# A graph network's expert layer: scatters and gathers of 25 blocks written out, a running sum by one scan, batch norm in five parts

## The chip, the cores and the metric

One Trainium2 chip, one of its cores. The metric is the device time of one execution of the whole kernel in microseconds (us). The engines are TensorE (PE; PEld is its weight load), VectorE (DVE), ScalarE (ACT), GpSimd (POOL) and SyncE (SP); each has its own instruction stream, and they meet through semaphores. DMAs are issued by SP and by POOL.

## The reference, cut to what matters

Four graph layers follow each other on 3125 nodes with 256 features, each added to its input: weighted means, a mixture of experts, four attention layers by angle, three graph attention layers. The change touches only the second. There `x` (3125 x 256) is what each node's feed-forward part starts from:

```python
logits = x @ Wg + bg                        # 64 experts
vals, idx = jax.lax.top_k(logits, TOP_K)    # 2 for each node
gates = jax.nn.softmax(vals, axis=-1)
order = jnp.argsort(e_flat)                 # nodes sorted by expert
rank = jnp.arange(N * TOP_K) - offs[e_s]    # place of a node within its expert
buf = zeros.at[slot].set(x[tok_s])          # rows to the experts
h1 = gelu(buf @ w1 + b1); h2 = h1 @ w2 + b2
core = zeros.at[tok_s].add(g_s[:, None] * y_s)   # rows back, weighted by the gate
y = x + core
mean = jnp.mean(y, axis=0)
var = jnp.mean((y - mean) ** 2, axis=0)
out = (y - mean) * jax.lax.rsqrt(var + BN_EPS) * gamma + beta
```

## The kernel before

The nodes lie in `NB = 25` blocks of 128 on the partitions; the last block has `LAST = 53` of them. `k.X` [128, 25, 256] is the sum that runs through the layers, `k.Y` of the same shape the `x` of this layer and later its `y`. A stage of the kernel is a block of code for all engines; between two blocks stands a barrier, so that a stage is as long as its slowest chain, and what one stage saves is not waited away in the next.

`route` (its first block) finds the two experts of each node on DVE, in tiles of 128 x 1600 (25 blocks x 64 experts). `cnt` holds a 1 where a node goes to an expert. TensorE multiplies it by `k.tri` (how many earlier nodes of the same block go there: `pre`) and by ones (how many of the block: `tot`). DVE copies both out of PSUM, and L1259 to L1262 is a loop in which each pass adds one block's totals to the sum of the blocks before, with a wait behind every addition. L1265 adds that sum to the rank. From the rank follow `slot_put` and `slot_get`, the row numbers in the experts' buffers in DRAM.

The second block of `route` scatters the rows of `Y` to the buffer `xbuf`. DVE copies a block's rows and its two columns of row numbers to a ring of `RING = 5` slots (L1332, L1333), because inside the loop the block number is a register; POOL issues two indirect DMAs for each block (L1342).

`experts` works on 112 tiles of 128 rows and writes `ybuf`. It is not changed.

`combine` is one block of code. DVE copies the row numbers of five blocks to `frm` (L1555), and the wait ahead of these copies is for all additions of the five blocks before. POOL gathers two rows for each node from `ybuf` to the ring `row` (L1544). DVE multiplies them by the gate and adds them to `Y` (L1561, two for each block). When all 50 additions are done, PE sums `Y` over the nodes by 25 products with ones (L1590, L1592); DVE takes the mean off `Y` (L1567), ACT squares `Y` to `acc` (L1581), PE sums the squares in the same way, DVE makes the factor `var` from it (L1569 to L1573), and three passes over 128 x 6400 elements end the layer: times `var` (L1574), plus beta (L1575, `aff[:, 1, :]`), and onto `X` (L1576). SP fetches gamma and beta at the start of the block (L1535). The next stage, a layer norm of `X` (L570), begins behind the barrier.

## Time and profile before

| | us |
|---|---|
| time, median of 2 runs | 8447.11 (8445.72 to 8448.5) |
| the profiled execution's own time | 8452.29 |
| span of the profiled execution | 8450.6 |
| busy: PE, DVE, POOL, ACT | 5775.2, 5350.2, 5261.2, 2998.2 |
| mean granted TensorE clock | 0.888 of full speed |

The span runs from the first to the last instruction. The busy times are sums over the whole span, and no engine is busy for more than 68% of it: the stages have different limits. The stages that the change touches lie between 2432 and 3198 us of the span, that is, 766 us with the experts (some 460 us) between them.

### The profile page before, as it was taken

To read this page: it belongs to the slowest core of one execution; us is meant where nothing else is said; L and a number is where in the kernel's file an instruction comes from. 1 tells how busy PE (TensorE), PEld (TensorE's weight loads), DVE (VectorE), ACT (ScalarE), POOL (GpSimd) and SP (SyncE) were. 2 spreads that over 40 slices of the span, in tenths; PEclk is the share of its full clock that TensorE was granted. 3 is DMA by queue.
4 is the path that set the end of the run, shared out by engine and by line. 5 is a ranking of instruction groups with operands and counts; after the bars stand their busy time and mean duration, and the time that the engine had idled before them with its cause. 6 is when DMAs were issued, how large, how long until landed. Compare 5 with 4: busy or idle time off the path is not lost. (4 is left out here: it accounts for less than half of the span.)

```text
span 8450.6 us, 153428 instructions
## 1 busy us (share of the span) xinstructions
PE 5775.2 (68%) x32873; PEld 4645.0 (55%) x33057; DVE 5350.2 (63%) x15356; ACT 2998.2 (35%) x7461; POOL 5261.2 (62%) x5324
## 2 busy tenths in 40 slices
PE   0005445546547945997997997898588878887886
PEld 0004435534336844776776776777366656655664
DVE  8003346664441227777776777777688868887888
ACT  0001100000012214444444444444466646655664
POOL 4777777757712125776776776776367646656764
PEclk9996677767778977999999999999799989999998
DMA  6001123323308942343443443443233323323332
GB/s 228 10 2 47 53 70 102 103 80 104 103 24 295 370 153 81 105 106 101 105 105 100 105 105 100 105 106 96 69 93 94 89 78 93 93 74 94 94 92 72
DMA packets 597889, 866.01 MB, mean 102 GB/s; under 512 B 273775, under 2 KB 412013, under 8 KB 596374
## 3 DMA queue, kind: packets, MB, share of 16 engines
q0 software_dynamic: 233280, 595.84, 25.6%
q1 hardware_dynamic: 364502, 269.16, 10.6%
q14 instruction: 90, 0.74, 0.0%
q8 instruction: 17, 0.28, 0.0%
HBM read 740.80 MB, written 125.75 MB: 103 GB/s over the span
## 5 line engine op out<-in xcount | busy, mean ns | idle before, releaser
L1766 POOL DMA_INDIRECT hs<-tab_agnn,rec x1952 | 1900.1, 973 | 653.6 <-issue 559.2
L2209 POOL DMA_INDIRECT hs<-tab_gat,rec x1464 | 1521.7, 1039 | 680.1 <-issue 417.2
L1832 DVE CUSTOM_DVE_ANT_0 prod<-psG,hs 128x256 f32<-128x256 f32 x1952 | 829.1, 481 | 404.9 <-DMA hs<-tab_agnn,rec 324.2
L1895 PE MATMUL psG<-HN,ohT 128*128 x3904 | 966.1, 391 | 12.8 <-DVE lg L1832 5.8
L2241 DVE TENSOR_REDUCE mt<-psL 128x2 f32<-128x1024 f32 x732 | 860.0, 1215 | 142.9 <-PE psL L2362 84.8
L1912 PE MATMUL psV<-hs,pr 128*128 128x258 f32 x3904 | 934.0, 383 | 0.0
L1895 PEld LDWEIGHTS psG<-HN,ohT 128*128 128x128 f32 x3904 | 710.6, 192 | 107.7 <-issue 20.3
L1849 ACT ACTIVATE prT<-cand,mn 128x512 f32<-128x512 f32 x488 | 352.4, 722 | 1170.2 <-DVE mn L1792 1157.9
L1912 PEld LDWEIGHTS psV<-hs,pr 128*128 128x128 f32 x3904 | 707.8, 191 | 80.9
L2378 PE MATMUL psV<-msg,oh 128*128 128x260 f32 x2928 | 730.4, 394 | 1.0 <-DVE msg L2286 0.6
L805 PE MATMUL psT<-ident,oh 128*128 128x128 f32 x416 | 101.6, 391 | 847.8 <-DVE oh L770 847.8
L2378 PEld LDWEIGHTS psV<-msg,oh 128*128 128x128 f32 x2928 | 580.0, 198 | 131.2 <-issue 9.1
L2362 PE MATMUL psL<-sT,sel 128*128 128x512 bf16 x1464 | 572.2, 391 | 15.8 <-DVE mt L2241 3.5
L805 PEld LDWEIGHTS psT<-ident,oh 128*128 128x128 f32 x416 | 65.2, 194 | 875.3 <-DVE oh L770 825.9
L2361 PE MATMUL psL<-neg,identb 128*128 128x512 bf16 x1281 | 500.7, 391 | 54.4 <-DVE mt L2241 54.4
L529 POOL DMA_INDIRECT rec_d<-R x392 | 397.8, 1015 | 215.1 <-issue 215.1
L657 POOL DMA_INDIRECT hs<-tab_gc,rec x416 | 406.9, 978 | 195.0 <-issue 122.9
L697 PE MATMUL ps<-hs,oh 128*128 128x256 f32 x832 | 316.8, 547 | 287.1 <-DMA hs<-tab_gc,rec 258.2
L875 POOL DMA_INDIRECT hs<-tab_bwd,rec x416 | 420.5, 1011 | 134.3 <-issue 125.4
L750 POOL DMA_INDIRECT fwd_d<-msg,rec x416 | 408.9, 983 | 141.9 <-issue 79.8
L2305 ACT ACTIVATE away<-iotas,rec 128x128 bf16 x1464 | 462.3, 386 | 92.3 <-DMA rec<-rec_d 57.5
L2286 DVE TENSOR_TENSOR msg<-hs,msg 128x1024 f32<-128x1024 f32 x366 | 451.4, 1233 | 5.4 <-ACT msg L2317 1.8
(346 smaller groups left out, 12120.4 us busy)
## 6 DMA issues: line engine op xcount, KB each, us to landing
w<-in_L_gnn_w SPq DMA_DIRECT2D x224, 512.0 KB, 6.0
hs<-tab_agnn,rec POOLq DMA_INDIRECT x1952
fwd_d<-acc SPq DMA_DIRECT2D x10, 2730.0 KB, 34.1
fw<-fwd_d SPq DMA_DIRECT2D x104, 260.0 KB, 2.8
hs<-tab_gat,rec POOLq DMA_INDIRECT x1464
rec<-rec_d SPq DMA_DIRECT2D x1166, 10.0 KB, 1.8
b<-in_L_gnn_b SPq DMA_DIRECT2D x113, 128.0 KB, 6.4
x<-xbuf SPq DMA_DIRECT2D x112, 128.0 KB, 6.0
```

The costliest lines, as they stand in the source:

```text
L875: nc.gpsimd.indirect_dma_start(out=hs[:, j, g, :], out_offset=None, in_=k.tab_bwd, in_offset=bass.IndirectOffsetOnAxis(ap=rec[:, j, g, 0:1 ...
L1766: nc.gpsimd.indirect_dma_start(out=hs[:, j, g, :], out_offset=None, in_=k.tab_agnn, in_offset=bass.IndirectOffsetOnAxis(ap=rec[:, j, g, 0: ...
L1832: ins = V.tensor_tensor_reduce(prod[:, h2, g, :], psG[:, bank(j2, half), m, :], hs[:, j2, g, 0:D], hs[:, j2, g, D:D + 1], 0.0, ALU.mult, A ...
L1895: mm = nc.tensor.matmul(psG[:, bank(j1, half), m, :], ohT[:, j1 % 2, 2 * half + m, :], pick(HN, b, slice(None)).rearrange("p a c -> p (a c ...
L1912: mm = nc.tensor.matmul(psV[:, j5 % 2, 0:cols], pr[:, j5 % 2, g, :], hs[:, j5, g, 0:cols], start=(g == 0), stop=(g == G - 1))
L2209: nc.gpsimd.indirect_dma_start(out=hs[:, j, g, :], out_offset=None, in_=k.tab_gat, in_offset=bass.IndirectOffsetOnAxis(ap=rec[:, j, g, 0:1 ...
L2241: V.tensor_reduce(mt[:, h2, m:m + 2], psL[:, m:m + 2, :], AX.X, ALU.max).then_inc(s_lt, 1)
L2286: V.tensor_tensor(hmsg[:, :, :, 0:C_HEAD], hrow[:, :, :, 0:C_HEAD], hmsg[:, :, :, C_HEAD].unsqueeze(3).to_broadcast([P, G, HEADS, C_HEAD]) ...
L2305: ins = nc.scalar.activation(away[:, j, g, :], nodes, ACT.Abs, bias=recf[:, j, g, 4:5], scale=-1.0)
L2361: nc.tensor.matmul(psL[:, m, :], k.identb[:, :], neg[:, h2, :], start=True, stop=False)
L2362: mm = nc.tensor.matmul(psL[:, m, :], sel[:, m, :], sT[:, h2, :], start=False, stop=True)
L2378: mm = nc.tensor.matmul(psV[:, h5, 0:W_GAT], oh[:, h5, g, :], msg[:, h5, g, :], start=(g == 0), stop=(g == G - 1))
```

## The change

In the first block of `route` the loop of additions goes. `tots` and `run` lie with the blocks innermost, DVE copies the totals there from PSUM in four pieces of 7, 7, 7 and 4 blocks, and one scan over 1600 elements multiplies the sum so far by `goes_on` (0 at an expert's first block, 1 elsewhere) and adds the next total. The scan's sum includes the block itself; `below = tri - 1` takes the place of `tri` and subtracts it again. `rank` is added up straight from PSUM, in four pieces. New at the start of the block are the instructions that write `below` and `goes_on`.

In the second block of `route` and in `combine` the loops over blocks are written out. The indirect DMAs take rows and row numbers from `Y`, `slot_put` and `slot_get` themselves; the copies of DVE are gone. In `combine` POOL waits, from the sixth block on, only for the two additions of the block five before.

Batch norm: beta is added to `X` at the start of `combine`. PE adds a block to the first sum as soon as the block's additions are done. Taking off the mean, squaring, the sum of squares, the product with `var` and the addition onto `X` go in five parts of five blocks.

```diff
-                c.mark(V.tensor_copy(sv(rank), pv(pre)))
-                c.mark(V.tensor_copy(sv(tots), pv(tot)))
-                with dve.Fori(0, NB) as b:
-                    V.tensor_tensor(pick(run, b + 1, slice(None)), pick(run, b, slice(None)), pick(tots, b, slice(None)),
-                                    ALU.add).then_inc(s_chain, 1)
-                    dve.wait_ge(s_chain, b + at + 1)
-                c.done(V.tensor_tensor(rank[:, :, :], rank[:, :, :], run[:, 0:NB, :], ALU.add))
+                c.mark(V.tensor_scalar(below[:, :], k.tri[:, :], 1.0, None, ALU.subtract))
+                c.done(V.memset(goes_on[:, :, :], 1.0))
+                c.mark(V.memset(goes_on[:, :, 0], 0.0))
...
+                for n in range(NC):
+                    c.mark(V.tensor_copy(tots[:, :, chunk(n)].rearrange("p e b -> p b e"), of(tot, n)))
+                dve.wait_ge(s_chain, c.n)
+                c.done(V.tensor_tensor_scan(flat(run), flat(goes_on), flat(tots), 0.0, ALU.mult, ALU.add))
+                for n in range(NC):
+                    c.mark(V.tensor_tensor(rank[:, chunk(n), :], of(pre, n), run[:, :, chunk(n)].rearrange("p e b -> p b e"), ALU.add))
...
+                for b in range(NB):
+                    if b >= RING:
+                        pool.wait_ge(s_put[b % RING], b // RING * 32)
+                    for m in range(TOP_K):
+                        nc.gpsimd.indirect_dma_start(
+                            out=k.xbuf, out_offset=bass.IndirectOffsetOnAxis(ap=k.slot_put[:, b, m:m + 1], axis=0),
+                            in_=k.Y[:, b, :], ...).then_inc(s_put[b % RING], 16)
...
+                for b in range(NB):
+                    if b >= RING:
+                        pool.wait_ge(s_add, TOP_K * (b - RING + 1))
+                    for m in range(TOP_K):
+                        nc.gpsimd.indirect_dma_start(
+                            out=row[:, b % RING, m, :], out_offset=None, in_=k.ybuf,
+                            in_offset=bass.IndirectOffsetOnAxis(ap=k.slot_get[:, b, m:m + 1], axis=0)).then_inc(s_get[b % RING], 16)
...
+                dve.wait_ge(s_gb, 32)
+                c.mark(V.tensor_tensor(k.X[:, :, :], k.X[:, :, :], mid(aff[:, 1, :], NB), ALU.add))
...
+                for n in range(RING):
+                    V.tensor_tensor(k.Y[:, parts[n], :], k.Y[:, parts[n], :], mid(mean[:, :], NB // RING), ALU.subtract).then_inc(s_part, 1)
...
-                c.done(V.tensor_tensor(Yf, Yf, mid(aff[:, 1, :], NB), ALU.add))
...
+                for n in range(RING):
+                    act.wait_ge(s_part, n + 1)
+                    nc.scalar.activation(k.acc[:, parts[n], 0:D], k.Y[:, parts[n], :], ACT.Square).then_inc(s_sq, 1)
...
+                for b in range(NB):
+                    pe.wait_ge(s_add, TOP_K * (b + 1))
+                    mm = total(0, b, k.Y)
```

On DVE in the first block of `route`, before:

```order
L1254 COPY rank<-pre 128x1600
L1255 COPY tots<-tot 128x1600
L1256 MEMSET run 128x64
L1259 UNCONDITIONAL_BRANCH
L1259 ISA
L1260 ISA
L1260 TENSOR_TENSOR run<-run,tots 128x64
L1262 REGISTER_ALU
L1259 REGISTER_ALU
L1259 COMPARE_AND_BRANCH
L1265 TENSOR_TENSOR rank<-rank,run 128x1600
```

and with the change:

```order
L1261 COPY tots<-tot 128x7x64 x3
L1261 COPY tots<-tot 128x4x64
L1263 SCALAR_TENSOR_TENSOR run<-goes_on,tots 128x1600
L1265 TENSOR_TENSOR rank<-pre,run 128x448 x3
L1265 TENSOR_TENSOR rank<-pre,run 128x256
```

The loop body, which ran 25 times, is gone, and the scan (it is listed under the name of its instruction family) stands between the four copies and the four additions; `rank` is written once instead of twice.

On POOL the scatter's stage, before (the ten DMAs are one pass of a loop of five):

```order
L1337 UNCONDITIONAL_BRANCH
L1337 ISA
L1342 DMA xbuf<-row,to 14336x256 x10
L1337 REGISTER_ALU
L1337 COMPARE_AND_BRANCH
```

and with the change:

```order
L1323 UNCONDITIONAL_BRANCH
L1329 DMA xbuf<-Y,slot_put 14336x256 x50
L1321 UNCONDITIONAL_BRANCH
```

The 50 scatters stand one behind the other, and read what DVE's copies used to stand between. The gathers of `combine` change in the same way (L1544 x10 in a loop to L1530 x50).

On DVE from the start of `combine` to its end, with the change:

```order
L1539 TENSOR_TENSOR X<-X,aff 128x6400
L1545 SCALAR_TENSOR_TENSOR Y<-row,gate,Y 128x256 x50
L1548 TENSOR_SCALAR mean<-ps 128x256
L1551 TENSOR_TENSOR Y<-Y,mean 128x1280 x5
L1553 TENSOR_SCALAR var<-ps 128x256
L1555 RECIPROCAL var<-std 128x256
L1556 TENSOR_TENSOR var<-var,aff 128x256
L1559 TENSOR_TENSOR Y<-Y,var 128x1280 x5
L1562 TENSOR_TENSOR X<-X,Y 128x1280 x5
```

where before, behind the additions, stood:

```order
L1566 TENSOR_SCALAR mean<-ps 128x256
L1567 TENSOR_TENSOR Y<-Y,mean 128x6400
L1569 TENSOR_SCALAR var<-ps 128x256
L1571 RECIPROCAL var<-std 128x256
L1573 TENSOR_TENSOR var<-var,aff 128x256
L1574 TENSOR_TENSOR Y<-Y,var 128x6400
L1575 TENSOR_TENSOR Y<-Y,aff 128x6400
L1576 TENSOR_TENSOR X<-X,Y 128x6400
```

The pass with beta moved from between the last two passes to ahead of all additions, and the other three are each five instructions.

## Rows read from the trace of the kernel before

**Rows 1.** Busy time by stretch: us, then each engine's busy us (instructions), clock, DMA

```profile
3045.50:3132.40 86.90, 0.00 (x0) 0.00 (x0) 28.17 (x75) 0.00 (x0) 49.41 (x50) 0.50 0.27 79
```

**Rows 2.** Timeline of DVE in the route: start, us, engine, line, operation, idle before

```profile
2466.56 1.82 DVE L1254 COPY rank<-pre 128x1600 f32<-128x1600 f32 x1 [6.32 <-PE tot L1304]
...
2471.44 0.22 DVE L1260 TENSOR_TENSOR run<-run,tots  x1 [0.56 <-DVE run L1260]
...
2491.26 0.20 DVE L1266 TENSOR_SCALAR ne<-run 128x64 f32<-128x64 f32 x1
```

**Rows 3.** Groups by line and shape: busy us, mean ns, idle before

```profile
L452 DVE TENSOR_TENSOR_SCAN scan<-onesj,carry,mask 128x296 f32<-128x296 f32 x50 | 39.0, 822 | 4.6 <-DVE prod L456 4.1 <-DVE R L472 0.5
L452 DVE TENSOR_TENSOR_SCAN scan<-onesj,offs,mask 128x96 f32<-128x96 f32 x50 | 18.2, 405 | 5.2 <-DVE carry L459 4.8 <-DVE prod L441 0.4
L664 DVE MEMSET acc<- 128x6500 f32 x1 | 5.5, 5475 | 12.6 <-issue 12.6
```

**Rows 4.** Timeline of DVE at the start of the experts

```profile
2587.68 0.61 DVE L1429 COPY b1T<-psx 128x256 f32<-128x256 f32 x1 [19.96 <-PE psx L1472]
...
2589.07 0.42 DVE L1443 COPY xT<-psx 128x256 f32<-128x256 f32 x1
```

**Rows 5.** Timeline at the start of the scatter's stage

```profile
2512.20 0.21 DVE L1290 TENSOR_TENSOR slot_put<-slotf,okf 128x50 int32<-128x50 f32 x1
...
2513.77 0.16 DVE L1333 COPY to<-slot_put 128x2 int32 x1
...
2514.87 1.02 POOL L1342 DMA_INDIRECT xbuf<-row,to  x1 [82.00 <-DVE to L1333]
```

**Rows 6.** Groups of the page's part 5: the scatters of the sorting stage

```profile
L529 POOL DMA_INDIRECT rec_d<-R x392 | 397.8, 1015 | 215.1 <-issue 215.1
```

**Rows 7.** Timeline of that stage

```profile
504.35 0.97 POOL L529 DMA_INDIRECT rec_d<-R  x1 [0.30 <-issue]
```

**Rows 8.** Groups by line between 3045 and 3133 us: the gathers

```profile
L1544 POOL DMA_INDIRECT row<-ybuf,frm x50 | 49.4, 988 | 45.1 <-DVE frm L1555 18.9 <-issue 13.7 <-SPq L1530 12.5
```

**Rows 9.** Timeline of combine: start, and the end of the first five blocks

```profile
3045.58 0.43 SPq L1535 DMA_DIRECT2D aff<-in_L_gnn_beta  x1
3046.58 1.01 POOL L1544 DMA_INDIRECT row<-ybuf,frm  x1 [12.55 <-SPq L1530]
...
3058.44 0.95 POOL L1544 DMA_INDIRECT row<-ybuf,frm  x1 [0.31 <-issue]
...
3061.98 0.49 DVE L1561 SCALAR_TENSOR_TENSOR Y<-row,gate,Y 128x256 f32 x1 [0.15 <-DVE Y L1561]
```

**Rows 10.** DMA issues: KB each, us from issue to landing

```profile
aff<-in_L_gnn_beta SPq DMA_DIRECT2D x1, 128.0 KB, 3.0
```

**Rows 11.** Timeline of graph attention: DVE and POOL at the same time

```profile
6498.79 1.22 DVE L2286 TENSOR_TENSOR msg<-hs,msg 128x1024 f32<-128x1024 f32 x1
6499.19 1.64 POOL L2209 DMA_INDIRECT hs<-tab_gat,rec  x1 [0.30 <-issue]
```

**Rows 12.** Timeline of the batch norm

```profile
3132.46 1.22 PE L1590 MATMUL ps<-Y,ones 53*128 53x256 f32 x2 [100.16 <-DVE Y L1561]
3146.55 0.42 DVE L1566 TENSOR_SCALAR mean<-ps 128x256 f32<-128x256 f32 x1 [14.14 <-PE ps L1592]
...
3159.46 1.22 PE L1590 MATMUL ps<-acc,ones 53*128 53x256 f32 x2 [12.94 <-ACT acc L1581]
...
3173.78 0.42 DVE L1569 TENSOR_SCALAR var<-ps 128x256 f32<-128x256 f32 x1 [19.94 <-PE ps L1592]
...
3183.86 6.83 DVE L1575 TENSOR_TENSOR Y<-Y,aff 128x6400 f32<-128x6400 f32 x1
```

**Rows 13.** Busy time by stretch, within the first sum on PE

```profile
3140.00:3147.00 7.00, 6.52 (x31) 5.40 (x29) 0.42 (x1) 0.00 (x0) 0.00 (x0) 1.00 0.00 0
```

**Rows 14.** Parts of five blocks in the attention by angle

```profile
3243.37 7.10 DVE L1698 TENSOR_TENSOR HN<-H,rnb 128x1280 f32<-128x1280 f32 x5
```

**Rows 15.** Groups of ACT between 3220 and 3245 us

```profile
L1706 ACT ACTIVATE HN<-H 128x1280 f32<-128x1280 f32 x5 | 6.4, 1270 | 3.7 <-DVE H L1683 3.5
```

More of the change, by code:

```diff
@@ L1190, in route @@
         rank = sb("rank", X3)
-        tots = sb("tots", X3)
-        run = sb("run", [P, NB + 1, EXPERTS])
+        tots = sb("tots", [P, EXPERTS, NB])
+        run = sb("run", [P, EXPERTS, NB])
+        goes_on = sb("goes_on", [P, EXPERTS, NB])
+        below = sb("below", [P, P])
         top = sb("top", [P, 2, NB])
@@ L1301, in _ @@
                 for n in range(NC):
-                    r = flat(cnt)[:, n * CH:(n + 1) * CH]
-                    nc.tensor.matmul(pre[:, n, 0:CH], k.tri[:, :], r, start=True, stop=True)
-                    mm = nc.tensor.matmul(tot[:, n, 0:CH], k.ones[:, 0:P], r, start=True, stop=True)
+                    r = cnt[:, chunk(n), :].rearrange("p b e -> p (b e)")
+                    nc.tensor.matmul(pre[:, n, 0:wide(n)], below[:, :], r, start=True, stop=True)
+                    mm = nc.tensor.matmul(tot[:, n, 0:wide(n)], k.ones[:, 0:P], r, start=True, stop=True)
                 mm.then_inc(s_pre, 1)
@@ L1512, in combine @@
         sem = lambda n: ctx.enter_context(nc.semaphore(tagged(nc, n)))
-        s_from = [sem(f"s_from{n}") for n in range(RING)]
         s_get = [sem(f"s_get{n}") for n in range(RING)]
@@ L1528, in combine @@
         ps = ctx.enter_context(nc.psum_tensor(tagged(nc, "ps"), [P, 2, 512], F32))
-        Yf = k.Y[:, :, :]
+        parts = [slice(n * (NB // RING), (n + 1) * (NB // RING)) for n in range(RING)]
         with nc.Block() as block:
@@ L1538, in _ @@
             def _(pool):
-                with pool.Fori(0, NB // RING) as i:
-                    for n in range(RING):
-                        pool.wait_ge(s_from[n], i + 1)
+                for b in range(NB):
+                    if b >= RING:
+                        pool.wait_ge(s_add, TOP_K * (b - RING + 1))
                         pool.sem_inc(s_gate, 1)
-                        for m in range(TOP_K):
-                            nc.gpsimd.indirect_dma_start(
-                                out=row[:, n, m, :], out_offset=None, in_=k.ybuf,
-                                in_offset=bass.IndirectOffsetOnAxis(ap=frm[:, n, m:m + 1], axis=0)).then_inc(s_get[n], 16)
+                    for m in range(TOP_K):
+                        nc.gpsimd.indirect_dma_start(
+                            out=row[:, b % RING, m, :], out_offset=None, in_=k.ybuf,
+                            in_offset=bass.IndirectOffsetOnAxis(ap=k.slot_get[:, b, m:m + 1], axis=0)).then_inc(s_get[b % RING], 16)
             @block.vector
@@ L1571, in _ @@
                 c.done(V.reciprocal(var[:, :], std[:, :]))
-                dve.wait_ge(s_gb, 32)
                 c.done(V.tensor_tensor(var[:, :], var[:, :], aff[:, 0, :], ALU.mult))
-                c.done(V.tensor_tensor(Yf, Yf, mid(var[:, :], NB), ALU.mult))
-                c.done(V.tensor_tensor(Yf, Yf, mid(aff[:, 1, :], NB), ALU.add))
-                c.done(V.tensor_tensor(k.X[:, :, :], k.X[:, :, :], Yf, ALU.add))
+                dve.wait_ge(s_part, RING)
+                for n in range(RING):
+                    V.tensor_tensor(k.Y[:, parts[n], :], k.Y[:, parts[n], :], mid(var[:, :], NB // RING), ALU.mult).then_inc(s_part, 1)
+                for n in range(RING):
+                    dve.wait_ge(s_part, RING + n + 1)
+                    c.mark(V.tensor_tensor(k.X[:, parts[n], :], k.X[:, parts[n], :], k.Y[:, parts[n], :], ALU.add))
             @block.scalar
             def _(act):
-                act.wait_ge(s_bn, 2)
-                nc.scalar.activation(k.acc[:, :, 0:D], Yf, ACT.Square).then_inc(s_sq, 1)
+                for n in range(RING):
+                    act.wait_ge(s_part, n + 1)
+                    nc.scalar.activation(k.acc[:, parts[n], 0:D], k.Y[:, parts[n], :], ACT.Square).then_inc(s_sq, 1)
                 act.wait_ge(s_bn, 3)
@@ L1586, in _, with total @@
             def _(pe):
[L1588 to L1593 removed]
+                def total(n, b, src):
+                    lo = LAST if b == NB - 1 else P
+                    return nc.tensor.matmul(ps[:, n, 0:D], k.ones[0:lo, 0:P], src[0:lo, b, 0:D], start=(b == 0), stop=(b == NB - 1))
+                for b in range(NB):
+                    pe.wait_ge(s_add, TOP_K * (b + 1))
+                    mm = total(0, b, k.Y)
+                mm.then_inc(s_sum, 1)
+                for b in range(NB):
+                    if b % (NB // RING) == 0:
+                        pe.wait_ge(s_sq, b // (NB // RING) + 1)
+                    mm = total(1, b, k.acc)
+                mm.then_inc(s_sum, 1)
 def attention_by_angle(nc, k, a):
```

65 lines of the change are left out of this document (16 added, 49 removed).

## The prediction

> **What bounds the kernel now.** The kernel is a row of stages with barriers between them, so I read the stages that the change touches one by one and ask in each for the chain that ends last. The view by stretches comes first [rows 1]: while rows come back from the experts (86.9 us), POOL is busy for 49.4 us, DVE for 28.2 us and PE not at all. Nobody is full; waits set the time. In the route the timeline shows a chain on DVE alone: from the copy of `pre` at 2466.56 to the first use of the finished sum at 2491.26, 24.7 us, most of it additions of 0.22 us with 0.5 to 0.6 us of waiting ahead of each [rows 2]. In the gathers the chain is POOL's: 50 DMAs of 0.988 us with 0.30 us of issue between them, and four waits of together 18.9 us for `frm` [rows 8]. Behind the last addition (3132.4) PE's sum, the mean, the squares, PE's second sum and three long passes of DVE stand one behind the other [rows 12].
>
> **The change part by part.**
>
> *Running sum.* 24.7 us go. New: four copies out of PSUM. A piece adds a fixed cost; 1600 elements took 1.82 us in one [rows 2], five pieces of 1280 took 7.10 us [rows 14] where 6400 in one took 6.83 [rows 12], so about 0.07 us for each cut: 2.0 us. Four additions from PSUM, the same 2.0. The scan: 296 elements took 822 ns and 96 took 405 [rows 3], so 2.09 ns an element, and 1600 make 3.5 us. With three waits 7.6 us. At the start of the block `below` and `goes_on` are new and nothing hides them, since the chain waits behind them: 6500 elements of memset took 5.48 us [rows 3], so 1600 take 1.4, and with two small instructions 1.8 us. Gain 24.7 - 7.6 - 1.8 = 15.3. The copies now write with a stride of 100 bytes, which no large instruction before does. The nearest row is a copy out of PSUM that writes with a stride of 16 bytes: 0.61 us for 256 elements against 0.42 with none [rows 4]; that may be the stride or not. Taken over to 1600 elements, for copies and additions, it costs at most 2.4 us; at least it costs nothing. I take nothing, and keep 2.4 for the range. PE's products have the same number of columns.
>
> *Scatter.* POOL sets the stage: one scatter follows the other, and DVE's copies run beside them. Scatters that are written out stand elsewhere in this kernel, 392 of them, and come 1.27 us apart, 0.97 busy and 0.30 issue [rows 6, 7]. So only the start counts. Before, the row numbers were copied at 2513.93 and POOL began 0.94 us later; the last instruction of the block before ended at 2512.41 [rows 5]. Without copies POOL starts from the barrier, which lies between, and still needs its 0.94 us: gain 1.0, bounds 0 and 1.5.
>
> *Gathers.* Waits of 18.9 us for `frm` go, and the ring does not take their place: a block is added 3.1 us after POOL has issued it (3059.39 to 3062.47, [rows 9]), and POOL comes back to the slot 10 us later. But DVE now begins with beta onto `X`, 6.83 us [rows 12], as soon as beta is there: 3045.58 + 3.0 = 3048.6 [rows 9, 10], until 3055.5. It has both inputs in SBUF. What such an instruction does to POOL stands in another stage: DVE's addition from 6498.79 to 6500.01, and a gather that was to start in the middle of it, at 6499.19, took 1.64 us instead of the 0.94 to 0.95 of its neighbours, so it was held until about 0.1 us before DVE's end [rows 11]. Here two or three gathers start before 3048.6; the next one is held until 3055.4, ends at 3056.35, and its successor starts at 3056.65. If three have started before, 46 remain: 46 x (0.988 + 0.304) = 59.4 [rows 8], the last ends at 3115.8. The additions end 3.1 us later in the shown five [rows 9], but in the last of the five fives 3.9 (the last gather there was issued from 3127.61 on), so I take 3.3: 3119.1, against 3132.4. With one gather more to go it is 3120.4. Middle of both: gain 12.6.
>
> The Trainium skill, "SBUF — State Buffer", section "Who interferes with whom", says that a DVE instruction with two SBUF inputs contends with a GpSimd instruction that reads SBUF, and that whichever comes first holds the port for its whole length. This case's trace agrees (1.64 us, rows 11). The same section reports that `tensor_tensor` did not stall DMA in an earlier probe; by that the hold would be nothing and the sum 5.8 us larger, which is the first rival below.
>
> *First sum.* PE added 25 blocks behind the last addition: 3132.46 to 3146.55, 14.1 us [rows 12]. Now 24 of them lie under the gathers (a block each 2.6 us, even at the low clock 0.9 us of PE) and the last costs the 1.22 us of its first pair [rows 12]: gain 12.8.
>
> *Squares.* Before, mean to `var` took 27.2 us [rows 12]. Now the first part is 0.42 + 1.5 us on DVE, 1.27 on ACT [rows 15], then PE's 25 blocks, which took 14.3 us [rows 12] and need about 2.1 (high clock) to 4.3 us (low) for a part, while the next part arrives after 1.4: PE never waits long, and its sum sets the end: 0.5 + 1.5 + 1.3 + 14.3 = 17.6. Gain 9.6. This keeps the clock's course: PE began at a low clock, and within the sum it was raised; in the first sum the mean of 3140 to 3147 was 1.00, that is 2.4 GHz, and 31 products took 6.52 us, 0.21 each [rows 13].
>
> *End.* The pass with beta, 6.83 us, is gone from here; two passes in five parts cost 0.27 us more each [rows 12, 14]: gain 6.3.
>
> Sum: 15.3 + 1.0 + 12.6 + 12.8 + 9.6 + 6.3 = 57.6 us. The profiled execution took 8452.3 us as a whole (span 8450.6): it would take 8394.7. The median of the two runs is 5.2 lower, so 8389.5 there.
>
> **The rivals.**
>
> - The hold does not happen, so that beta's pass is free. The gather that starts at about 3049.6 ends at 3050.6 and not at 3056.35: 5.8 us more gain, 8384. Against it: the gather that was held in the other stage [rows 11]. Chance 0.12.
> - PE stays at the low clock for the sum of squares, since its work before is now in small pieces, and five-block parts may leave gaps. Each product would take 0.43 instead of 0.21, 50 of them 21.3 instead of 14.3: 7 us less gain, 8396. Against it: from the first square on PE has a queue. Chance 0.12.
> - The strided copies or the scan cost more, or part of a saved wait comes back in a barrier or in the next layer's start: 5 to 15 us less, 8395 to 8405. Chance 0.12.
> - Slower than before: instructions that are written out are fetched from DRAM once each, while a loop's are at hand. If POOL stalls at this, 100 indirect DMAs pay. It decides from 0.58 us for each DMA (57.6 / 100); at 1 us each the time is 8389 + 100 = 8489. For it speaks only that the issue in rows 6 has a mean of 0.55 us, with the waits for the sorting in it. Against it: 392 written-out scatters at 1.27 us [rows 7]. Chance 0.02, also for ending above 8447.
> - The change does not do what it says (the wait for the ring bites as `frm` did): POOL would wait again for 18.9 us, 8408. Against it: the 10 us of slack. Chance 0.02.
>
> **How the numbers follow.** The forecast has chance 0.6, with 8380 to 8399 as its own range (stride 2.4, start 1.5, one gather 1.3, the clock's rise a few us earlier or later, 3 us between runs). The range that holds 8 in 10 takes in the first two rivals and most of the third: 8376 to 8404. A measurement of this kernel can tell about 2% from no change, which is 169 us. All of what these stages could give is less: the touched stretches sum to about 25 + 73 + 87 + 65 us, and POOL's 100 DMAs alone keep 127 of them. Faster by over 2%: 0.01. Slower by over 2%: 0.01. Within: 0.98.
>
> **What would show it.** In the profile of the changed kernel: a scan of 3.5 us between four copies and four additions, each group 2.0 us; scatters at 1.27 us with DVE idle; beta onto `X` at about 3032 (3048.6 less the 16.3 us saved before), and one gather beside it of 5 to 7 us instead of 1; no wait of POOL for DVE's additions; the mean 1.3 us behind the last addition; `var` 17.6 us behind the mean; 14.2 us for the last ten passes. A mean gather duration of 1 us with none above 2 would prove the hold wrong; a gap above 0.5 us between written-out DMAs would prove the price of written-out code wrong; and if the stages save 57 us but the time does not, what lies behind them has changed, which no row here foretells.

## The result, and the profile after

The changed kernel takes 8361.55 us (median of 2 runs, 8360.1 to 8363.0) against 8447.11 before: 0.9898 of it, 95% interval 0.988 to 0.9915. That is 85.6 us less, where 57.6 were forecast; the forecast of 8389.5 (8376 to 8404) lay 28 us above the measured time. The profiled executions, which the sum was made against, differ by 92.2 us in their spans.

The page of after, its first lines (span; busy time of each engine, share, instructions):

```profile
span 8358.4 us, 152930 instructions
## 1 busy us (share of the span) xinstructions
PE 5760.2 (69%) x32873; PEld 4634.0 (55%) x33057; DVE 5311.7 (64%) x15276; ACT 3000.4 (36%) x7465; POOL 5337.3 (64%) x5324
```

The route, as in [rows 2]: a timeline of DVE with start, us, engine, line, operation, names and the idle time ahead.

```profile
2465.49 2.98 DVE L1261 COPY tots<-tot 128x448 f32<-128x448 f32 x4 [7.56 <-PE tot L1305]
2468.50 3.49 DVE L1263 TENSOR_TENSOR_SCAN run<-goes_on,tots 128x1600 f32<-128x1600 f32 x1
2472.03 3.15 DVE L1265 TENSOR_TENSOR rank<-pre,run 128x448 f32<-128x448 f32 x4
2475.22 0.22 DVE L1267 TENSOR_SCALAR ne<-run 128x64 f32<-128x64 f32 x1
```

From the first copy to the first use of the sum 9.73 us pass, before 24.7. The scan takes the 3.5 us forecast; the copies and additions take 2.98 and 3.15, not 2.0 each.

The start of the scatters, as in [rows 5]:

```profile
2496.16 0.21 DVE L1291 TENSOR_TENSOR slot_put<-slotf,okf 128x50 int32<-128x50 f32 x1
2497.96 1.01 POOL L1329 DMA_INDIRECT xbuf<-Y,slot_put  x1 [69.39 <-PEq L1321]
2499.28 1.00 POOL L1329 DMA_INDIRECT xbuf<-Y,slot_put  x1 [0.31 <-issue]
```

The start of the gathers, as in [rows 9]:

```profile
3029.38 0.43 SPq L1521 DMA_DIRECT2D aff<-in_L_gnn_beta  x1
3029.72 1.01 POOL L1530 DMA_INDIRECT row<-ybuf,slot_get  x1 [11.89 <-POOLq L1376]
3031.04 0.99 POOL L1530 DMA_INDIRECT row<-ybuf,slot_get  x1 [0.30 <-issue]
3032.34 0.95 POOL L1530 DMA_INDIRECT row<-ybuf,slot_get  x1 [0.30 <-issue]
3032.64 6.82 DVE L1539 TENSOR_TENSOR X<-X,aff 128x6400 f32<-128x6400 f32 x1 [16.07 <-DMA aff<-in_L_gnn_beta]
3033.59 6.70 POOL L1530 DMA_INDIRECT row<-ybuf,slot_get  x1 [0.30 <-issue]
3039.39 1.00 DVE L1545 SCALAR_TENSOR_TENSOR Y<-row,gate,Y 128x256 f32<-128x256 f32 x2
...
3040.59 0.94 POOL L1530 DMA_INDIRECT row<-ybuf,slot_get  x1 [0.30 <-DVE Y L1545]
```

The hold of the forecast is there in full: the fourth gather starts while DVE adds beta and takes 6.70 us. And the batch norm, as in [rows 12] and [rows 14]:

```profile
3100.50 1.00 DVE L1545 SCALAR_TENSOR_TENSOR Y<-row,gate,Y 128x256 f32<-128x256 f32 x2 [2.30 <-DMA row<-ybuf,slot_get]
...
3102.81 0.42 DVE L1548 TENSOR_SCALAR mean<-ps 128x256 f32<-128x256 f32 x1 [1.31 <-PE ps L1577]
3103.27 7.10 DVE L1551 TENSOR_TENSOR Y<-Y,mean 128x1280 f32<-128x1280 f32 x5
...
3119.88 0.42 DVE L1553 TENSOR_SCALAR var<-ps 128x256 f32<-128x256 f32 x1 [9.51 <-PE ps L1577]
...
3123.10 7.10 DVE L1559 TENSOR_TENSOR Y<-Y,var 128x1280 f32<-128x1280 f32 x5
3130.12 7.09 DVE L1562 TENSOR_TENSOR X<-X,Y 128x1280 f32<-128x1280 f32 x5
```

The mean starts 1.31 us behind the last addition, `var` 17.07 us behind the mean.

To place the 92.2 us I cut every trace at the starts of certain instructions of POOL: its first iota of the route, the first scatter, the first gather of `combine`, the iota behind it, the first gather of the attention by angle, the iota behind its last gather, and the first and last gathers of the graph attention. The short stretches ahead of "by angle" and on both sides of "graph att." are in no column, and so the delay of p2_before_delay, which lies in the first of them, isn't either. The table holds all kernels of this study. "Place" is the number of VectorE instructions that the built program holds ahead of the attention by angle; "gather" is the mean of one gather of the graph attention. The medians of one row are to be read by the ratio to the kernel before on the same chip, since chips differ by some 14 us (before had medians from 8447 to 8461); ratios in brackets are of a single run. The stages are those of one profiled execution for each kernel: after and p4_after are the same kernel, and differ by 4.2 us in the attention by angle and 3.5 us in the graph attention, so less than some 5 us in these two columns says nothing by itself.

| kernel | ahead of route | route | scatter, experts | combine | by angle | graph att. | gather, ns | place | median, us | ratio |
|---|---|---|---|---|---|---|---|---|---|---|
| before | 2432.4 | 82.4 | 531.7 | 176.8 | 2700.7 | 2329.7 | 1039 | 1342 | 8447.1 | 1 |
| after | 2428.1 | 69.8 | 531.8 | 133.1 | 2686.6 | 2311.9 | 1095 | 1326 | 8361.5 | 0.9898 |
| e1_route | 2434.8 | 70.7 | 530.8 | 176.9 | 2700.2 | 2330.5 | 1044 | 1341 | 8446.2 | 0.9983 |
| e2_loops | 2436.2 | 82.2 | 530.5 | 156.0 | 2694.1 | 2309.1 | 1095 | 1315 | 8405.7 | 0.9936 |
| e3_batchnorm | 2427.8 | 83.9 | 541.6 | 146.2 | 2685.6 | 2318.5 | 1100 | 1354 | 8418.4 | 0.9952 |
| e4_beta_psum | 2430.6 | 69.1 | 530.2 | 127.5 | 2706.7 | 2312.5 | 1096 | 1327 | 8372.7 | 0.9897 |
| p1_before_pad12 | 2429.9 | 83.9 | 531.2 | 175.7 | 2686.8 | 2313.4 | 1095 | 1354 | 8421.8 | 0.9968 |
| p2_before_delay | 2429.1 | 82.3 | 529.8 | 175.5 | 2699.7 | 2333.5 | 1040 | 1342 | 8460.8 | 1.0012 |
| p3_after_pad14 | 2428.9 | 69.9 | 529.9 | 132.2 | 2695.2 | 2330.1 | 1045 | 1342 | 8387.7 | 0.9930 |
| p4_after | 2431.0 | 69.2 | 531.1 | 133.0 | 2690.8 | 2308.4 | 1094 | 1326 | 8362.8 | 0.9899 |
| q1_poolpad12 | 2434.6 | 83.0 | 531.1 | 177.7 | 2704.2 | 2333.7 | 1044 | 1342 | 8456.9 | 0.9994 |
| q2_beta_psum_pad | 2433.6 | 69.3 | 531.4 | 127.0 | 2688.5 | 2320.9 | 1099 | 1354 | 8369.5 | 0.9891 |
| q3_after_pad26 | 2436.4 | 69.2 | 531.1 | 133.1 | 2690.0 | 2318.9 | 1100 | 1354 | 8378.1 | 0.9905 |
| q4_route_twins | 2433.2 | 73.4 | 531.3 | 132.7 | 2692.3 | 2312.8 | 1096 | 1334 | 8374.2 | (0.9897) |
| t1_beta_psum_pad5 | 2430.4 | 69.3 | 529.9 | 127.5 | 2689.4 | 2333.3 | 1038 | 1334 | 8378.2 | 0.9919 |
| t2_before_pad4 | 2429.1 | 83.0 | 531.4 | 177.5 | 2690.0 | 2343.1 | 1028 | 1346 | 8453.5 | (1.0007) |
| t3_before_pad8 | 2427.0 | 83.0 | 532.1 | 176.9 | 2689.6 | 2313.7 | 1097 | 1350 | 8418.9 | (0.9966) |
| t4_after_pad10 | 2427.6 | 69.2 | 532.1 | 132.8 | 2684.8 | 2311.9 | 1094 | 1338 | 8354.9 | (0.9890) |
| u1_before_pad12_experts | 2430.2 | 83.9 | 532.0 | 177.7 | 2687.0 | 2314.0 | 1095 | 1354 | 8425.4 | (0.9960) |
| u2_beta_psum_pad9 | 2434.7 | 69.9 | 530.7 | 127.6 | 2689.8 | 2313.2 | 1097 | 1338 | 8365.8 | 0.9890 |

Route and combine give 12.6 and 43.7 us, with the short stretches behind them (0.6) 56.9 us: the forecast's 57.6. The other 35 us (of which the medians, 85.6 us apart instead of 92.2, keep some 29) lie where no line was changed (1.0 us the other way behind the last gather): 4.3 ahead of the route (this stretch varies between 2427.0 and 2436.4 us over all these kernels without a pattern), 14.1 in the attention by angle and 17.8 in the graph attention. The experiments are about these last two.

What differs inside the graph attention can be read from groups by line of DVE and POOL between 5960 and 8270 us (busy us, mean ns of one, idle ahead). The kernel before:

```profile
L2279 DVE TENSOR_SCALAR t<-t 128x16 f32<-128x16 f32 x345 | 78.7, 228 | 0.1
L2209 POOL DMA_INDIRECT hs<-tab_gat,rec x1400 | 1457.3, 1041 | 650.3 <-issue 400.7 <-DVE msg L2286 195.4 <-DMA rec<-rec_d 54.2
```

The kernel after, run once more on the chip of p1 to p3 (p4_after):

```profile
L2273 DVE TENSOR_SCALAR t<-t 128x16 f32<-128x16 f32 x360 | 60.7, 169 | 0.1
L2203 POOL DMA_INDIRECT hs<-tab_gat,rec x1462 | 1600.1, 1094 | 577.6 <-issue 439.5 <-DVE msg L2280 74.3 <-DMA rec<-rec_d 54.5
```

The window cuts off the last 64 gathers of before, whose stage ends later; over all 1464 gathers of each kernel the waits for `msg` are 208.7 and 74.3 us. The same instructions fall in one of two patterns. In the short one gathers last longer (they are held by `msg`), the small `t` is not slowed, and POOL waits for DVE 134 us less. In the long one gathers are shorter, and `t` is slowed in part of the turns: it takes over 0.26 us in 96 of 366 turns of before and in 1 of p4_after.

### The profile page after: what moved, and what is told of

Read it like the earlier page. It is cut to its first block and busy times, and to the rows that moved or that the text cites. A ratio compares the mean times of both kernels' runs of the same rounds, so it can differ in the third digit from the quotient of the medians.

```text
span 8358.4 us, 152930 instructions
## 1 busy us (share of the span) xinstructions
PE 5760.2 (69%) x32873; PEld 4634.0 (55%) x33057; DVE 5311.7 (64%) x15276; ACT 3000.4 (36%) x7465; POOL 5337.3 (64%) x5324
## 5 line engine op out<-in xcount | busy, mean ns | idle before, releaser
L2203 POOL DMA_INDIRECT hs<-tab_gat,rec x1464 | 1602.6, 1095 | 577.3 <-issue 432.3
L2299 ACT ACTIVATE away<-iotas,rec 128x128 bf16 x1464 | 462.3, 386 | 91.6 <-DMA rec<-rec_d 56.9
```

What stands on the lines that cost most here:

```text
L2203: nc.gpsimd.indirect_dma_start(out=hs[:, j, g, :], out_offset=None, in_=k.tab_gat, in_offset=bass.IndirectOffsetOnAxis(ap=rec[:, j, g, 0:1 ...
L2299: ins = nc.scalar.activation(away[:, j, g, :], nodes, ACT.Abs, bias=recf[:, j, g, 4:5], scale=-1.0)
```

## Experiments

### One part of the change at a time

e1_route has only the change of `route`, e2_loops only the written-out scatters and gathers, e3_batchnorm only the change of the batch norm with its pass of beta ahead of the additions; each the lines of the diff above.

> Only the first block of the route is changed: the scan in place of the loop of additions; scatter, gathers and batch norm are as before. Stage theory: the touched stage gives what it gave in the full change, about 11.7 us (12.6 with the scatter's start, less 0.9), and nothing else moves: 8435 us. Rival 1, the stages behind it with unchanged code depend on when they start: the attention stages then differ from those of before by up to 32 us in either direction, and the graph attention shows one of two patterns of POOL and DVE (the product L2279 at 231 or at 168 ns). Rival 2, the extra time of the full change comes from where the code lies: with DVE's and POOL's code nearly where it was, the attention stages stay within 3 us of before.

Measured: 0.9983 (0.9973 to 0.9993) of before. The route is 11.7 us shorter, no other stage moves by more than 2.4 us.

> Only the scatters and gathers are written out, without the copies of DVE; route and batch norm are as before. Stage theory: 0.9 us at the scatter, four waits of 4.7 us and 0.7 us at the start of the gathers, and no long addition of DVE that holds a gather: 20 us less, 8427 us. Rival 1 (start time decides in the attention stages): those change by some other sum than in the full change. Rival 2 (where the code lies): POOL's code has moved by the same 120 instructions as in the full change, so the attention stages give back the same 28 to 32 us: 8397 us.

Measured: 0.9936 (0.9919 to 0.9952), some 53 us less. Combine is 20.8 us shorter as expected; 20.6 us more are gone in the graph attention and 6.6 in the attention by angle.

> Only the batch norm is changed (beta onto X at the start, sums and passes in parts); the loops with their copies stay. Stage theory: behind the last addition 29.6 us less (12.8, 10.2 and 6.6 in the profile of the full change), but the first copies of row numbers now stand behind beta's pass, which begins when beta has landed: the gathers start 10 us later. Net 20 us less, 8427 us. Rival 1: the attention stages move by a sum of their own. Rival 2: PE's and ACT's code decides, then the 28 to 32 us appear here.

Measured: 0.9952 (0.9936 to 0.9969), some 41 us less. The profiled execution took 8403.0 us, the other three 8417.5 to 8420.4: its stages are those of an execution some 15 us shorter than the rest, and no trace shows where the others spent that. Combine from its first gather is 30.6 us shorter, but this gather starts 9.9 us later, because the index copies of the loop now stand behind beta's pass on DVE. A timeline of e3_batchnorm:

```profile
3045.56 6.83 DVE L1553 TENSOR_TENSOR X<-X,aff 128x6400 f32<-128x6400 f32 x1 [15.80 <-DMA aff<-in_L_gnn_beta]
3052.30 0.44 DVE L1558 COPY frm<-slot_get 128x2 int32 x5
3053.36 1.01 POOL L1544 DMA_INDIRECT row<-ybuf,frm  x1 [22.33 <-DVE frm L1558]
```

So the pass ahead of the additions pays only together with gathers that need nothing of DVE. The attention stages give 15.1 and 11.2 us more in this execution. Each part does in its own stage what the sum said; two of the three also shorten the attention stages, and POOL's code, which e3_batchnorm leaves as it was, can't be the reason for both.

### The hold by DVE's addition

```diff
-                c.mark(V.tensor_tensor(k.X[:, :, :], k.X[:, :, :], mid(aff[:, 1, :], NB), ALU.add))
+                V.tensor_copy(beta[:, 0:D], aff[:, 1, :]).then_inc(s_gb, 1)
+                dve.wait_ge(s_gb, 33)
+                c.mark(V.tensor_tensor(k.X[:, :, :], k.X[:, :, :], mid(beta[:, 0:D], NB), ALU.add))
```

`beta` is a tile in PSUM, so the long pass has one input in SBUF instead of two.

> The changed kernel, but beta is copied to PSUM first (one more copy of 0.3 us on DVE), and the long addition onto X reads one input from SBUF and one from PSUM. If the hold comes from the two inputs in SBUF, no gather beside it takes more than 1.3 us (6.70 us in the changed kernel), and the additions end 5.5 us earlier: 8356 us. If the hold comes from the length or the traffic of the pass, one gather still takes 6 to 7 us: 8362 us.

The timeline of e4_beta_psum at the place where after had its gather of 6.70 us:

```profile
3033.18 6.82 DVE L1542 TENSOR_TENSOR X<-X,beta 128x6400 f32<-128x6400 f32 x1
3033.76 0.95 POOL L1531 DMA_INDIRECT row<-ybuf,slot_get  x1 [0.30 <-issue]
3035.02 0.94 POOL L1531 DMA_INDIRECT row<-ybuf,slot_get  x1 [0.30 <-issue]
...
3038.78 0.94 POOL L1531 DMA_INDIRECT row<-ybuf,slot_get  x1 [0.30 <-issue]
```

Five gathers run beside the same 6.82 us at their full pace, and combine is 5.6 us shorter than in after (127.5 against 133.1). The hold is shown, cause and size. But the kernel stood at 0.9897 (0.9881 to 0.9914), no better than after: its attention by angle took 2706.7 us, 20 more than after's and 16 more than that of p4_after.

### Start time, or the place of code

Two theories for the attention stages. Start time: they begin 61 us earlier, and so at another phase of something. Place: an instruction more or less on an engine ahead of them moves the code of their loops. Against start time spoke that all three layers of an execution show the same pattern although they begin some 800 us apart. The pads are

```diff
+                for n in range(12):
+                    nc.vector.memset(pad[:, n:n + 1], 0.0)
```

behind DVE's copies of the scatter stage (before) or as a block of their own beside the scatters (after); in p2 two `nc.gpsimd.memset` of the tiles `HN` and `hs` stand behind the iota ahead of the attention by angle.

> The kernel before with one thing added: 12 VectorE memsets of one column (128 x 1) of a tile that nothing reads, behind the copies of the scatter stage, where VectorE idles some 10 us while GpSimd ends its scatters. They cost the stage nothing. They move the VectorE code of all later stages on by 12 instructions, as the batch norm in parts did (1342 VectorE instructions stand ahead of the attention by angle in the kernel before, 1341 in e1_route, 1354 in e3_batchnorm, 1326 in after, 1315 in e2_loops). Theory of code position (the attention stages with unchanged code run in one of two patterns, and which one depends on where the VectorE code lies): the graph attention falls from 2330 us to 2312 to 2319 us and its L2209 gathers rise from a mean of 1039 to about 1096 ns; time about 0.998 of before. Theory of start time (the pattern depends on how much earlier the stages start): nothing changes, 1.000 of before, gathers 1039 ns.

> The kernel before with two GpSimd memsets (6400 and about 6200 elements a partition) behind the iota ahead of the attention by angle: GpSimd comes some 11 us later to that stage (its memset of 6500 took 5.5 us), and all behind it with it. No VectorE, ScalarE or TensorE instruction is added. Theory of code position on VectorE: graph attention as before, 2330 us, gathers 1039 ns, time = before + 9 to 11 us (1.0012 of before). Theory of start time: the attention stages change by several us in length, graph attention by up to 20.

> The kernel after with 14 VectorE memsets of one column and the block that holds them beside the scatters, so that again 1342 VectorE instructions stand ahead of the attention by angle, as in the kernel before. They lie beside 63 us of scatters. Theory of code position on VectorE, if position alone decides: the graph attention goes back from 2312 to about 2330 us and its gathers to a mean of 1039 ns; the time is 18 us above that of the kernel after on this chip (ratio to before about 0.992). Theory of start time, or of another engine's code: it stays at 2312 us, gathers 1096 ns, ratio as after.

> The kernel after once more, on the same chip as p1 to p3, so that their stages can be held against it: ratio to before about 0.990; graph attention 2312 us with gathers of 1096 ns. How far its attention by angle differs from the 2686.6 us of the first profile shows what of that stage's differences between kernels is the chip's and not the kernel's.

Measured: p1 0.9968 (0.9956 to 0.9981), 29 us less with 12 instructions more; graph attention 2313.4 us, gathers 1095 ns; and 13.9 us less in the attention by angle. p2 1.0012 (1.0003 to 1.0022), +10 us, all patterns as before. p3 0.9930 (0.9913 to 0.9946), 25 us over p4 with 0.9899 (0.9882 to 0.9915); graph attention back at 2330.1 us, gathers 1045 ns. Against start time speak p2, where 11 us of delay change no pattern, and p1, where it changes although the attention by angle starts within 4 us of before (3246.9 against 3250.3); place holds in both directions. (In the attention by angle p3 is 4.4 us over p4, hardly more than the 4.2 us between the two profiles of one kernel.) The two patterns in detail, the same turn of four gathers (the 40th of the first layer); p4_after first, then p3_after_pad14:

```profile
6216.23 0.16 DVE L2249 TENSOR_TENSOR raw<-smax,sp 128x4 f32 x1
6216.34 0.18 DVE L2252 TENSOR_TENSOR raw<-hs,psQ 128x16 f32<-128x16 f32 x1
...
6216.80 0.96 POOL L2203 DMA_INDIRECT hs<-tab_gat,rec  x1 [0.30 <-issue]
...
6217.31 0.17 DVE L2273 TENSOR_SCALAR t<-t 128x16 f32<-128x16 f32 x1
...
6217.96 1.22 DVE L2280 TENSOR_TENSOR msg<-hs,msg 128x1024 f32<-128x1024 f32 x1
6218.07 1.94 POOL L2203 DMA_INDIRECT hs<-tab_gat,rec  x1 [0.30 <-issue]
...
6220.31 0.94 POOL L2203 DMA_INDIRECT hs<-tab_gat,rec  x1 [0.30 <-issue]
```

```profile
6219.89 0.16 DVE L2255 TENSOR_TENSOR raw<-smax,sp 128x4 f32 x1
6220.13 0.18 DVE L2258 TENSOR_TENSOR raw<-hs,psQ 128x16 f32<-128x16 f32 x1
...
6220.46 0.95 POOL L2209 DMA_INDIRECT hs<-tab_gat,rec  x1 [0.30 <-issue]
...
6221.06 0.36 DVE L2279 TENSOR_SCALAR t<-t 128x16 f32<-128x16 f32 x1
...
6221.71 1.27 DVE L2286 TENSOR_TENSOR msg<-hs,msg 128x1024 f32<-128x1024 f32 x1
6221.72 0.95 POOL L2209 DMA_INDIRECT hs<-tab_gat,rec  x1 [0.30 <-issue]
6223.79 0.94 POOL L2209 DMA_INDIRECT hs<-tab_gat,rec  x1 [1.12 <-DVE msg L2286]
```

In p4 `t` comes half a microsecond into a gather and takes 0.17 us, `msg` follows and holds the last gather of the turn to 1.94 us; the next starts 2.24 us behind its start. In p3 `t` comes 0.60 us into the gather and takes 0.36, `msg` starts 0.01 us before the gather, which is not held, and POOL then waits 1.12 us for `msg`. This one turn does not show the loss (from the last gather to the next start p3 is even 0.17 us shorter); it shows that about 0.1 us decides which engine waits.

The traces hold two more facts on this. The first: over all turns of before, p3 and p4, a `t` that starts up to 0.52 us into a gather takes 0.17 us (0.18 at most), and one that starts 0.53 to 0.76 us into it ends 0.94 to 0.95 us behind the gather's start, when the gather ends too (it takes 0.41 us at 0.53, 0.35 at 0.59, 0.23 at 0.71; three at the border of 0.53 still take 0.17); in p4 35 turns have it at 0.51, just short of that. The second is that the loop body holds six turns of four gathers, and that every kernel of the long pattern has in the same one of them a delay of 0.10 to 0.13 us between two instructions of VectorE ahead of `t`. It is between the two `raw` in p3 (0.24 us from start to start where p4 has 0.11), between the second `raw` and `leaky` in before, e1, p2 and q1, between `smax` and `raw` in t2, between the first `t` and `df` in t1. In each of the three layers it comes back pass after pass, equal to about 0.01 us (16 passes of each layer). No kernel with the short pattern has more than 0.01 us there (median of a layer); e3, q2 and q3, with 2318 to 2321 us, have 0.11 us in another turn. So the pattern is not a chance state that the loop keeps: each pass makes it anew, and six turns take 35.4 us in p4 and 35.7 in p3.

From its eighth gather on to the 479th a layer takes 686.1 to 686.6 us in p4 and 691.7 to 692.7 in p3.

### Which engine, and do the memsets themselves do it

> The kernel before with 12 GpSimd memsets of one column at the start of the experts' part, where GpSimd waits anyway: as p1_before_pad12, but on the other engine. 1342 VectorE instructions stand ahead of the attention by angle as before, GpSimd's code lies 12 further on. Theory that VectorE's place alone decides: graph attention about 2330 us, its L2209 gathers a mean of 1039 ns, time 1.000 of before. Theory that any engine's place does it (or where the whole program lies in memory): graph attention 2312 us and gathers near 1100 ns, time about 0.997 of before as p1_before_pad12.

> The kernel after with 26 one-column VectorE memsets instead of the 14 of p3_after_pad14: 1354 VectorE instructions ahead of the attention by angle. Place theory: the fast pattern of graph attention (about 2312 us, gathers 1100 ns) although p3_after_pad14, with 12 memsets fewer, had the slow one (2330 us); ratio 0.990 against 0.993. If instead any block with memsets beside the scatters did the harm in p3_after_pad14: 2330 us again, ratio 0.993.

> The kernel before with the 12 one-column VectorE memsets of p1_before_pad12, but put at the start of the experts' part (VectorE waits there for a load) and not behind the scatters: the same number ahead of the attention stages, from another spot. One look. If the place of the attention's VectorE code decides, the graph attention is as in p1_before_pad12: 2313 us, gathers 1106 ns. If it is something the memsets do where they stand, it may be 2330 us and 1039 ns again. (t1_beta_psum_pad5 was slow at the count of 1334 at which q4_route_twins was fast, so the count alone, taken at the start of the attention by angle, is not a rule across kernels that differ elsewhere.)

Measured: q1 0.9994 (0.9984 to 1.0004), long pattern as before: moving POOL's code by 12 instructions, the one step tried, does nothing. q3 0.9905 (0.9889 to 0.9922), gathers 1100 ns: 12 memsets more than in p3 at the same spot bring the short pattern back, here in a variant of 2318.9 us. u1: the 12 memsets of p1 moved to another stage give what p1 gave (2687.0 and 2314.0 us against 2686.8 and 2313.4). So it is not what the memsets do where they stand, but that VectorE instructions stand ahead. The number alone does not settle it, as the next runs show.

### How fine it acts, and the better kernel

t2 and t3 are p1 with 4 and 8 memsets, t4 is p3 with 10, q2, t1 and u2 are e4_beta_psum with 25, 5 and 9.

> The kernel before with 4 one-column VectorE memsets behind the copies of the scatter stage: place 1346. One look, for the pattern of graph attention: 2330 us with gathers of 1039 ns (slow, as at 1341 and 1342) or 2312 us with gathers near 1100 ns (fast, as at 1354). The theory of place says that it is one or the other and the same in all three layers; it does not foretell where between 1342 and 1354 the border lies.

> As t2_before_pad4 with 8 memsets: place 1350. One look. With t2_before_pad4 it shows whether the step between 1342 (slow) and 1354 (fast) is one border (slow-slow-fast, slow-fast-fast) or whether the pattern goes to and fro within a few instructions (fast-slow).

> The kernel after with 10 one-column VectorE memsets and their block beside the scatters: place 1338, between 1334 (q4_route_twins, fast) and 1341 (e1_route, slow). One look. One border between: the graph attention takes either 2312 or 2330 us, the same in all three layers; the time follows it, 8360 or 8380 us.

> e4_beta_psum (the kernel after with beta copied to PSUM) with 25 one-column VectorE memsets and their block beside the scatters, so that 1354 VectorE instructions stand ahead of the attention by angle, as in p1_before_pad12 and e3_batchnorm, whose attention by angle took 2686 us; e4_beta_psum, at 1327, had 2707 us. If the place of VectorE's code took away what the PSUM copy had brought: attention by angle about 2687 us, graph attention 2309 to 2313 us, and the gathers of the combine 5.6 us shorter than in the kernel after (127.5 us to the iotas): 8355 us, ratio 0.989. If the PSUM tile itself is what costs in the stages behind: attention by angle 2705 us again, ratio 0.991.

> e4_beta_psum with 5 one-column VectorE memsets and their block beside the scatters: 1334 VectorE instructions ahead of the attention by angle, the place at which q4_route_twins had the fast pattern of graph attention (2312.8 us) and 2692 us of attention by angle. Place theory: combine to iotas 127.0 us (6 less than after), attention by angle about 2690 us and not the 2707 us of e4_beta_psum, graph attention 2309 to 2313 us: ratio about 0.988, the fastest of all. Without a hold on place: as e4_beta_psum, 2707 us there and 0.990.

> e4_beta_psum with 9 one-column VectorE memsets beside the scatters, the count of t4_after_pad10 (1338), at which both attention stages were short (2684.8 and 2311.9 us). Combine to iotas 127.3 us (6 us under after). Which pattern it takes can't be told from the count (t1 missed): with the short ones in both stages 0.988 to 0.989 of before, the fastest so far; with the slow graph attention 0.991; with the long attention by angle of e4_beta_psum 0.990.

Measured: before with 0, 4, 8 and 12 memsets takes 2329.7, 2343.1, 2313.7 and 2313.4 us in the graph attention; 4 instructions make it 13 us longer, 4 more 29 us shorter. t4 at 1338 is short in both stages (8354.9 us, one run).

t1 missed. At the count of 1334, where q4_route_twins (below) has the short pattern, it has the long one (1038 ns, 2333.3 us): 0.9919 (0.9902 to 0.9935). So the count at the start of the attention stages is no rule by itself. The delay in the loop tells the two apart: t1 has 0.10 us more between `t` and `df` than q4 in its median. But its attention by angle took 2689.4 us: the 2706.7 of e4_beta_psum went with place, not with PSUM.

q2 against q3, equal in place and run on the same chip: combine 127.0 against 133.1, the whole 8369.5 against 8378.1 us, 0.9891 (0.9875 to 0.9908) against 0.9905. u2, with the short patterns in both stages: 0.9890 (0.9874 to 0.9907). The copy of beta to PSUM is worth its 6 us in combine wherever it was measured. In the whole kernel only the pair of q2 and q3 shows it: at the place of u2 (1338) t4, without the copy, has 0.9890 too, in its one run. u2 is no better than after (0.9898) by more than the interval.

### The strides of the route

```diff
+                for n in range(NC):
+                    c.mark(V.tensor_copy(tmp[:, chunk(n), :], of(tot, n)))
+                dve.wait_ge(s_chain, c.n)
+                for n in range(NC):
+                    c.mark(V.tensor_tensor(tmp[:, chunk(n), :], of(pre, n), tmp[:, chunk(n), :], ALU.add))
```

> The kernel after with twins in the route: behind the scan, four copies of the same PSUM counts written without the transposition (contiguous) and four adds that read and write contiguous rows. One look, for the mean of each shape. Theory that the strides are what the two steps cost over the prediction: the plain copies take 0.50 us each and the plain adds about 0.5 us (2.0 us for each group of four) beside 0.75 and 0.79 us for the strided ones. Theory that four smaller instructions or PSUM reads cost it: the twins take as long as the strided ones. The stage gets 4 to 5 us longer. With 1334 VectorE instructions ahead of the attention by angle it is also one more place for the graph attention's pattern; no theory here foretells which.

The timeline of DVE in q4_route_twins; L1265 and L1268 are the twins without strides of L1261 and L1271:

```profile
2469.99 2.98 DVE L1261 COPY tots<-tot 128x448 f32<-128x448 f32 x4 [6.98 <-PE tot L1311]
2473.00 3.49 DVE L1263 TENSOR_TENSOR_SCAN run<-goes_on,tots 128x1600 f32<-128x1600 f32 x1
2476.53 2.02 DVE L1265 COPY tmp<-tot 128x448 f32<-128x448 f32 x4
2478.58 2.02 DVE L1268 TENSOR_TENSOR tmp<-pre,tmp 128x448 f32<-128x448 f32 x4
2480.64 3.15 DVE L1271 TENSOR_TENSOR rank<-pre,run 128x448 f32<-128x448 f32 x4
```

A stride of 100 bytes costs 0.96 us for 1600 elements written and 1.13 for 1600 read, 0.6 and 0.7 ns an element; the cut in four costs the 0.2 us forecast.

## Why the prediction was wrong, point by point

**Running sum**, 15.3 forecast, 11.7 measured (e1 alone, and after). The chain shrank by 15.0 with the strides in it: four copies and four additions took 6.13 us instead of 4.0, the 2.1 us of strides that the forecast named with a bound of 2.4 and took as nothing. The remaining 3.3 us lie ahead of the chain: about 2 are the new work at the start (1.8 forecast), and 1.2 are the copies' wait for PE, 7.56 us instead of the 6.32 of [rows 2], which the forecast put at nothing ("the same number of columns").

**Scatter**, 1.0 forecast, 0.87 measured: the first scatter starts 1.59 us behind the end of `slot_put`, before 2.46. Written out, they keep their 1.3 us pitch, and the stage with the experts is as long as before (531.8 against 531.7). The rival of slow written-out code has fallen.

**Gathers**, 12.6 forecast, 14.0 measured (first gather to the end of the last addition, 85.8 to 71.8). Three gathers start before the hold, as forecast, and the hold is 6.70 us. The forecast for this case alone, three gathers ahead of the hold, was 13.3. The rest is pitch: later gathers take 0.94 to 0.95 us, not the mean of 0.988. That mean held eleven gathers of 1.04 to 1.20 us which had started while one of DVE's additions (0.48 us, `row` and `Y`) was running, the small form of the same hold; in after none of the later gathers is over 1.0 us. 46 times 0.04 make 1.8 us, so the other sizes were a little too kind. The rival without a hold has fallen. The Trainium skill, "SBUF — State Buffer", section "Who interferes with whom", states that a DVE instruction with two inputs in SBUF contends with a GpSimd instruction that reads SBUF, and one with at most one, outside the performance modes that the page sets apart, does not. The trace agrees on both sides, with 6.70 us in after and 0.95 in e4_beta_psum; the earlier probe that this section tells of, in which `tensor_tensor` did not stall DMA, is not borne out here.

**First sum**, 12.8 forecast and measured (14.14 to 1.31). **Squares**, 9.6 forecast, 10.2 measured (27.2 to 17.07): PE begins with a granted clock of 0.50 and has 0.82 on average over its second sum (the view by stretches of after):

```profile
3029.30:3101.70 72.40, 29.46 (x49) 12.18 (x49) 30.95 (x51) 0.00 (x0) 53.20 (x50) 0.50 0.32 94
3106.10:3119.90 13.80, 13.71 (x50) 11.10 (x50) 4.29 (x5) 6.36 (x5) 0.00 (x0) 0.82 0.00 1
```

So it leaves 1.2 GHz within that sum, and the rival of a low clock has fallen. **End**, 6.3 forecast, 6.6 measured.

The terms come to 56.2 us against 57.6. That is closer than the terms are one by one: 3.6 us too much in the running sum stand against 2.3 us too little in gathers, squares and end. The step that failed is none of them; it is the one that makes the sum the time of the program: span minus 57.6, as if stages with unchanged code kept their length. They did not. By the profiles 31.9 us came from the two attention stages, and p1 gets 30.2 us there (13.9 and 16.3) without any of the change, p3 gives 26.1 back against p4 with all of it. The last sentence of its "What would show it" named this case, but gave it no size and no chance, and the range ended 14.5 us short of the result.

What remains open: why VectorE has the delay of 0.10 to 0.13 us in the loop of the graph attention, and how the instructions ahead set its spot. The traces show that it is there, where, and that the patterns go with it, and not the fetch of an instruction. The attention by angle I have not read for such a delay; there 6.6 of the 14 us lie within the layers (their 9th to 480th gathers sum to 2427.1 us before, 2420.5 after) and 10.3 from there to the first gather of the next layer (163.6 against 153.3), of which the first eight gathers of the layers take 3.4 back; I have not taken this further apart. The 4.3 us ahead of the route were not studied.

## What to carry to other kernels

Where two engines share a long loop and each can hold the other, its length can have several values, and a small edit ahead of it can switch them: here 13 and 29 us in 2330 by four memsets each (single runs). So an edit of a few tenths of a per cent is judged by the time of its own stage, and the rest against a twin with a few idle instructions more or less; otherwise a good edit is thrown away (e4_beta_psum) or a lucky one kept. And a long DVE addition beside indirect gathers did better with its second input in PSUM: no gather was held, 6 us of 133.

## What was not expected of the hardware

- The number of VectorE instructions ahead of a loop changed its length: graph attention 2308 to 2343 us, attention by angle 2685 to 2707 us, the graph attention's pattern the same in every layer and again in the second profile of the same kernel (2311.9 and 2308.4 us). Twelve instructions more on GpSimd changed nothing (2333.7 us), nor did 11 us of delay (2333.5 us).
- A `tensor_scalar` of 16 elements took 0.17 us when it started up to 0.52 us into an indirect gather of 0.95 us, and until the gather's end when it started at 0.53 to 0.76 us (graph attention of before, p3 and p4).
- A DVE access to SBUF with a stride of 100 bytes, the other side in PSUM, cost 0.6 ns more an element when written and 0.7 when read, on 1.26 ns for the plain one (2.02 us for 1600 elements, cut in four).
- `tensor_tensor_scan` took 3.49 us for 1600 elements, 2.18 ns each, nearly twice the 1.14 of an addition (1.83 us, L1265 of before).
